# Recurrent stage of an AdaLN / attention / FFN kernel: skip term and residual as products on TensorE, copies and first taps on ScalarE, start and tail reordered

## What is computed

```python
xn = h * rsqrt(mean(h * h, -1) + 1e-6) * rms_w
proj = xn @ in_proj_W.T + in_proj_b                 # z, K (two parts), V
vc = causal depthwise conv of V, 4 taps
u = silu(vc + conv_b)
dyn, sel_B, sel_C, seldt, beta, gates = u @ ...     # per head: the "heads"
Y = scan over the 1024 steps (2x2 rotation, rank-1 correction)
y = sum(Q * Y)
y = groupnorm(y) over 16 channels x all steps, times gn_w, plus gn_b
y = y * silu(z)
y = y + D * u                                       # the skip term
branch = h + y @ out_W.T                            # h is folded elsewhere
x = x + branch                                      # the residual
```

## Time and profile before

| | us |
|---|---|
| median of 3 runs (lowest to highest) | 2272.09 (2267.52 to 2276.97) |
| the profiled execution | 2275.35 |
| its span in the profile | 2273.6 |
| TensorE, VectorE, ScalarE busy in the span | 1917.5, 1596.7, 886.0 |

### The profile page before, as it was taken

The page is one execution under the profiler, slowest core; times in us unless marked ns, Lnnn a source line. Parts: engine busy times, 40 slices in busy tenths (PEclk is TensorE's granted clock), DMA queues, the critical chain, the costliest instruction groups (busy, mean ns, idle before and its releaser), DMA issues. The chain is left out here.

```text
span 2273.6 us, 28338 instructions
## 1 busy us (share of the span) xinstructions
PE 1917.5 (84%) x9864; PEld 1237.0 (54%) x9864; DVE 1596.7 (70%) x3420; ACT 886.0 (39%) x1659; POOL 461.5 (20%) x350
## 2 busy tenths in 40 slices
PE   7999998999999987956865377455889999999997
PEld 4544443788888855433433233232354444379997
DVE  4688873545444354789999999999467888266775
ACT  2366764222232222530122111101326776446775
POOL 1021210433230030001001101110011221114775
PEclk9899988999999998978887788777988999979999
DMA  6033332211010011000000000000032342138885
GB/s 182 13 73 65 66 64 80 84 56 56 32 42 0 0 56 66 26 1 10 10 1 9 19 0 10 9 0 0 24 57 43 74 82 49 35 116 238 231 235 121
DMA packets 60158, 132.73 MB, mean 58 GB/s; under 512 B 18952, under 2 KB 29960, under 8 KB 57216
## 3 DMA queue, kind: packets, MB, share of 16 engines
q1 hardware_dynamic: 50688, 118.17, 19.2%
q0 software_dynamic: 8832, 12.16, 3.2%
q10 hardware_dynamic: 512, 0.79, 0.2%
HBM read 91.27 MB, written 10.98 MB: 45 GB/s over the span
## 5 line engine op out<-in xcount | busy, mean ns | idle before, releaser
L810 DVE CUSTOM_DVE_ANT_0 pair<-pair,a_mask 128x512 f32<-128x512 f32 (+3 forms) x768 | 407.3, 588 | 108.6 <-PE pair L621 106.4
L776 ACT ACTIVATE a_prob<-pair 128x512 f32<-128x512 f32 (+3 forms) x768 | 330.3, 491 | 174.7 <-PE pair L648 172.6
L621 PE MATMUL pair<-a_kx,a_qx 48*128 48x512 f32 (+3 forms) x768 | 246.6, 411 | 15.9 <-DVE a_mx_raw L810 8.9
L648 PE MATMUL pair<-a_qx,a_kx 64*128 64x512 f32 (+3 forms) x768 | 248.3, 432 | 9.2 <-ACT a_prob L776 9.2
L648 PEld LDWEIGHTS pair<-a_qx,a_kx 64*128 64x128 f32 x768 | 119.0, 197 | 186.7 <-ACT a_prob L776 135.6
L1079 DVE TENSOR_TENSOR m_h<-pair,m_g 128x512 f32<-128x512 f32 x96 | 66.3, 691 | 205.0 <-PE pair L870 202.1
L1466 PE MATMUL pair<-h_stream,r_w_kz 128*128 128x512 f32 x192 | 103.7, 694 | 118.8 <-DVE r_region L1872 113.4
L868 PE MATMUL pair<-m_x_hi,m_w_lo 128*128 128x512 f32 x448 | 178.8, 399 | 19.3 <-DVE m_w_lo L1042 6.4
L662 PE MATMUL pair<-a_prob,a_v 128*32 128x512 f32 (+3 forms) x1536 | 177.6, 536 | 6.5 <-ACT a_prob L776 4.0
L869 PE MATMUL pair<-m_x_hi,m_w_hi 128*128 128x512 f32 x448 | 177.6, 396 | 0.0
L870 PE MATMUL pair<-m_x_lo,m_w_hi 128*128 128x512 f32 x448 | 177.1, 395 | 0.0
(11 more groups left out here) (323 smaller groups left out, 4080.2 us busy)
## 6 DMA issues: line engine op xcount, KB each, us to landing
mx_raw<-in_L_ffn_experts SPq DMA_DIRECT2D x69, 512.0 KB
comp_or_raw<-in_L_cond_experts SPq DMA_DIRECT2D x18, 1024.0 KB, 5.0
a_factor<-a_inverses SPq DMA_DIRECT2D x56, 128.0 KB, 2.7
a_qx<-comp_or_raw SPq DMA_DIRECT2D x52, 96.0 KB, 2.7
a_qx<-a_comp SPq DMA_DIRECT2D x52, 96.0 KB, 2.7
a_kx<-comp_or_raw SPq DMA_DIRECT2D x24, 192.0 KB, 4.5
a_kx<-a_comp SPq DMA_DIRECT2D x24, 192.0 KB, 4.5
r_w_ring<-in_r_q_w SPq DMA_DIRECT2D x8, 512.0 KB, 3.9
```

The lines of the kernel that those rows point to most:

```text
L621: nc.tensor.matmul(first_bank[t % FR][:, 0:c1 - c0], qx[r, m % 2, a // 2, i * P:(i + 1) * P], kx[r, m % 3, a // 2, c0:c1], start=True, sto ...
L648: nc.tensor.matmul(score_bank[t % SR][:, q0:TT], kx[r, n % 3, a // 2, j * P:(j + 1) * P], qx[r, n % 2, a // 2, h * TT + q0:(h + 1) * TT], ...
L776: nc.scalar.activation(prob[:, i % RING, a, q0:TT], score_bank[t % SR][:, q0:TT], ACT.Exp, scale=SCALE).then_inc(s["b_exp"], 1)
L810: nc.vector.tensor_tensor_reduce(out=first_bank[t % FR][:, 0:cols], in0=first_bank[t % FR][:, 0:cols], in1=mask[:, m0:m0 + cols], scale=1. ...
```

## The change

- **Skip term.** L1964 goes, so a gate is one operation and counts `fin` once. In unit 4 ScalarE scales a copy of the output weights by D (`w_skip`, four operations), and TensorE adds D * u through it: four more products per result tile.
- **Residual.** One more product per tile, identity times x (read by step), starts each sum. ScalarE copies the finished tile back into x, by step, in place of VectorE's add. For batch 1 the identity and skip products are tiles of their own, `("skip", 1, o, h)`, late in unit 5's ring, copied to x by ScalarE; the y part is still added at the end.
- **First taps.** `first_tap` on ScalarE, right after `evict_v`, replaces L1755.
- **Start.** Two of the four squares go to VectorE. **Tail.** `result(0, 0)`, `result(0, 1)`, `result(1, 0)` are issued when half 0 of the last outputs is read, ahead of the first group sum; `result(1, 1)` between the group sums.

```diff
@@ -1258,7 +1258,7 @@
 READ = 2 * HALF_T
-TAPS = 1 + 2 * (TG - 1)
+TAPS = 2 * (TG - 1)
@@ -1281,6 +1281,8 @@
             tiles += [("out", 0, o, h) for o in range(KD) for h in halves]
+        if r == KI + 1:
+            tiles += [("skip", 1, o, h) for o in range(KD) for h in halves]
         rings.append(tiles)
@@ -1288,7 +1290,7 @@
 RING_ALL = [tile for tiles in RINGS for tile in tiles]
-BY_DVE = ("gn1", "out")
+BY_DVE = ("gn1",)
@@ -1308,7 +1310,7 @@
     names = ("norms const vload hload sload kload qload oload sq gp ga gd rc xn pad acc u h1 h2 cb cd cp x1 qc d1 ya "
-             "as st fin ai oadd omm dt dt2 tail").split()
+             "as st fin ai oadd omm dt dt2 tail tap skip_w").split()
     s = {n: c.sem(f"r_{n}") for n in names}
@@ -1341,6 +1343,7 @@
         w_o = tmp[:, 0:4, :].rearrange("p a t -> p (a t)").rearrange("p (k m) -> p k m", k=KI)
+        w_skip = tmp[:, 4:8, :].rearrange("p a t -> p (a t)").rearrange("p (k m) -> p k m", k=KI)
         values = [*c.quad, *[bank[:, :] for bank in c.bank]]
@@ -1429,7 +1432,7 @@
                     for i, tile in enumerate(tiles):
-                        if (tile[0] == "out") != late:
+                        if (tile[0] in ("out", "skip")) != late:
                             continue
@@ -1481,11 +1484,17 @@
                             b, o, h = which
-                            pe.wait_ge(s["oload"], 16)
-                            pe.wait_ge(s["fin"], 2 * KI)
+                            pe.wait_ge(s["skip_w"], KI)
+                            nc.tensor.matmul(bank.rearrange("p (g i) -> p g i", g=2), c.ident[:, :], by_step(c.x, b, o, h),
+                                             start=True, stop=False)
                             for k in range(KI):
-                                last = nc.tensor.matmul(bank, w_o[:, k, o * P:(o + 1) * P], ybuf[:, k, half(h)],
-                                                        start=k == 0, stop=k == KI - 1)
+                                last = nc.tensor.matmul(bank, w_skip[:, k, o * P:(o + 1) * P], u[:, b, k, half(h)],
+                                                        start=False, stop=what == "skip" and k == KI - 1)
+                            if what == "out":
+                                pe.wait_ge(s["fin"], KI)
+                                for k in range(KI):
+                                    last = nc.tensor.matmul(bank, w_o[:, k, o * P:(o + 1) * P], ybuf[:, k, half(h)],
+                                                            start=False, stop=k == KI - 1)
                         last.then_inc(s["gp"], 1)
@@ -1539,19 +1548,22 @@
                 def result(k, o):
-                    pe.wait_ge(s["fin"], 2 * (KI + k + 1))
+                    pe.wait_ge(s["fin"], KI + k + 1)
                     for h in range(HALF_T):
...
+                pe.wait_ge(s["d1"], (NU - 1) * READ + 2)
+                result(0, 0)
+                result(0, 1)
+                result(1, 0)
                 pe.wait_ge(s["d1"], NU * READ)
-                result(0, 0)
                 group_sum(("gn1", NU - 1))
-                result(0, 1)
+                result(1, 1)
                 group_sum(("gn2", NU - 1))
-                for k in range(1, KI):
+                for k in range(2, KI):
                     for o in range(KD):
@@ -1573,6 +1585,11 @@
                                              bias=in_bias[:, m:m + 1]).then_inc(s["ga"], 1)
+
+                def first_tap(b, m):
+                    act.wait_ge(s["ga"], taken(("v", b, m, HALF_T - 1))[1])
+                    nc.scalar.activation(u[:, b, m, :].rearrange("p (g i) -> p g i", g=TG), vpad[b][:, m, :, 1:GT + 1], ACT.Identity,
+                                         scale=vecs[:, m, 3:4]).then_inc(s["tap"], 1)
@@ -1591,7 +1608,7 @@
                     if r >= 2:
-                        act.wait_ge(s["fin"], 2 * (r - 1))
+                        act.wait_ge(s["fin"], r - 1)
                     for h in range(HALF_T):
@@ -1674,18 +1691,19 @@
-                for b in range(B):
-                    for k in range(KD):
-                        nc.scalar.activation(squares[:, b * KD + k, :], seq(c.h, b)[:, k, :], ACT.Square).then_inc(s["sq"], 1)
+                for k in range(KD):
+                    nc.scalar.activation(squares[:, k, :], seq(c.h, 0)[:, k, :], ACT.Square).then_inc(s["sq"], 1)
                 act.wait_ge(s["norms"], 2 * 16)
...
                     evict_v(0, m)
+                    first_tap(0, m)
                 evict_k(0)
...
                     evict_v(1, m)
+                    first_tap(1, m)
                     silu_u(0, m)
@@ -1707,6 +1725,17 @@
                         normalize(r - 1)
+                    if r == KI:
+                        act.wait_ge(s["oload"], 16)
+                        for k in range(KI):
+                            nc.scalar.activation(w_skip[:, k, :], w_o[:, k, :], ACT.Identity, scale=vecs[:, k, 7:8])\
+                                .then_inc(s["skip_w"], 1)
+                    if r in (KI, KI + 1):
+                        for o in range(KD):
+                            for h in range(HALF_T):
+                                tile = ("out", 0, o, h) if r == KI else ("skip", 1, o, h)
+                                nc.scalar.activation(by_step(c.x, tile[1], o, h), tile_in(tile).rearrange("p (g i) -> p g i", g=2),
+                                                     ACT.Copy).then_inc(s["ga"], 1)
                     for i in LATER_HEADS.get(r, ()):
@@ -1732,7 +1761,7 @@
                         if r and h == HALF_T - 1:
-                            pool.wait_ge(s["fin"], 2 * r)
+                            pool.wait_ge(s["fin"], r)
                         tt(ybuf[:, m, half(h)], coef[:, 2, half(h)], coef[:, 5, half(h)], ALU.add).then_inc(s["ya"], 1)
@@ -1750,12 +1779,12 @@
                 def convolve(b, m):
-                    dve.wait_ge(s["ga"], taken(("v", b, m, HALF_T - 1))[1])
                     v, out = vpad[b][:, m, :, :], u[:, b, m, :].rearrange("p (g i) -> p g i", g=TG)
-                    ts(out, v[:, :, 1:GT + 1], vecs[:, m, 3:4], None, ALU.mult).then_inc(s["acc"], 1)
+                    dve.wait_ge(s["tap"], b * KI + m + 1)
                     for back in range(1, TG):
                         w = vecs[:, m, 3 - back:4 - back]
-                        dve.wait_ge(s["acc"], (b * KI + m) * TAPS + 2 * back - 1)
+                        if back > 1:
+                            dve.wait_ge(s["acc"], (b * KI + m) * TAPS + 2 * (back - 1))
                         for to, src in ((out[:, back:TG, :], v[:, 0:TG - back, 1:GT + 1]),
@@ -1960,9 +1989,6 @@
                     tt(ybuf[:, m, :], ybuf[:, m, :], zbuf[:, r % 2, :], ALU.mult).then_inc(s["fin"], 1)
-                    dve.wait_ge(s["fin"], 2 * r + 1)
-                    stt(out=ybuf[:, m, :], in0=u[:, b, m, :], scalar=vecs[:, m, 7:8], in1=ybuf[:, m, :],
-                        op0=ALU.mult, op1=ALU.add).then_inc(s["fin"], 1)
@@ -1980,13 +2006,6 @@
                         down(level)
-                        if r == KI and level == 1:
-                            for o in range(KD):
-                                for h in range(HALF_T):
-                                    dve.wait_ge(s["gp"], made(("out", 0, o, h)))
-                                    x = by_step(c.x, 0, o, h)
-                                    tt(x, ring_bank(("out", 0, o, h)).rearrange("p (g i) -> p g i", g=2), x, ALU.add)\
-                                        .then_inc(s["gd"], 1)
                         if later and level == 4:
@@ -2002,6 +2021,9 @@
+                for k in range(KD):
+                    h1 = seq(c.h, 1)[:, k, :]
+                    nc.vector.tensor_tensor(squares[:, KD + k, :], h1, h1, ALU.mult).then_inc(s["sq"], 1)
                 for b in range(B):
@@ -2030,6 +2052,7 @@
                 gate(NU - 1)
+                dve.wait_ge(s["ga"], taken(("skip", 1, KD - 1, HALF_T - 1))[1])
                 for o in range(KD):
```

## The result

The changed kernel measured 2284.04 us (median of 18 runs, 2278.04 to 2295.59), the kernel before 2276.02 in 18 runs beside it; the ratio is 1.0051, 95% interval [1.003, 1.0072], where the two medians alone stand 8.0 us or 0.35% apart. Both intervals lie above 1, so the changed kernel is slower, by half to three quarters of a per cent. The 2283.3 us of the forecast lies close, but by its steps it was worse than that looks, as the stage shows.

What follows compares the result with a forecast made beforehand. TensorE was taken to bound the joints and VectorE the scan between them. Terms 9.6 + 2.9 - 0.3 + 2.1 - 3.1 = +11.2 us on the 2272.09 us median gave 2283.3 us, range 2274 to 2292.

Steps and rivals of the forecast that it cites:

- the bound and its places: Joints belong to TensorE, the scan between to VectorE; VectorE waits some 18 us in unit 4, 5 in unit 5.
- Rival 4: Unit 4: added products hide in TensorE's idle time, -9.7 us or -14.5 with joints, 2257 to 2262 us; chance 0.03.
- units 4 and 5: Added products delay the half-1 queries VectorE waits for: +9.6 us in unit 4, +2.9 us in unit 5.
- all added products have this size: Units 4 and 5: every product added to TensorE is priced as 512 columns of fp32, 0.86 us each.
- rival 1: Units 4 and 5: identity products' reads by step slow, +3.5 us, +6.9 at a doubling, 2287 to 2290; chance 0.31.
- Start: Stage start: taps on ScalarE delay head products 1.1 us, low clock costs 1.8, one tap gives -0.75; sum +2.1 us.
- rival 2: Stage start: the clock holds and the pause stays short, -2.2 us instead of +2.1, 2279 us; chance 0.12.
- Other joints and tail: Four lighter gates at other joints give -0.3 us; fewer result products left at the end give -3.1 us.
- The 4.6 us at the low clock: Tail: first group sum stands behind six result products, low clock for the first 4.6 us; 1590.3 against 1590.38.
- The sum: Whole kernel: 9.6 + 2.9 - 0.3 + 2.1 - 3.1 = +11.2 us, put on the median: 2283.3 us.
- 0.43 us a product: Behind unit 5: without the 13.43 us pause, 40 spread records take 0.43 us a product, not 11.38 us for 20.

Runs made afterwards that it cites:

- the second set: The changed kernel, unedited, measured again against the kernel before: 2290.03 us (12 runs; before 2276.76), ratio 1.0074.
- the kernel of 699.8 us: Kernel before with split squares, one first tap on ScalarE, unit 4's adds moved down, reordered end, POOL's gate wait lifted; ratios 0.9985 and 0.996.

## Why the prediction was right or wrong

- **Right: the bound and its places.** The joints are TensorE's (the run without D * u), the added products all stand ahead of a reader that waits, and the two waits lie where they were put. Without the step VectorE's wait in unit 4 is 17.94 us for 18 forecast. Rival 4, that the products hide, needed 14 us or less; the queue is 35.
- **Wrong in size: units 4 and 5.** The step that failed is "all added products have this size", 0.86 us. It holds for the 48 skip and y products; the eight identity products read by step and take 1.79. Unit 4 is +13.1 for +9.6, unit 5 +7.0 for +2.9. Both differences (3.5 and 4.1) are nearly four times 0.93, 3.7. This was rival 1 at its doubling, with 6.9 us forecast and 6.7 to 7.0 measured. The chance of 0.31 was too low: the only rows by step there were, VectorE's, said 1.5, and the forecast took 1. The Trainium skill (SBUF — State Buffer, Door 1: The DMA port swizzle) wants two hits on a 16-byte line, and by that rule such a read is slow, as it was: 1.79 us for 0.86. The same section lets fp32 be read by a step of four for free, which these numbers contradict; the measurement decides. Whether missing second hits are the cause, no run here shows.
- **Start, +1.0 for +2.1.** Right in kind: the mean comes 1.5 us earlier (2.44 us into the stage for 3.95), ScalarE's chain then holds the heads up, the pause is 4.33 us (5 forecast), and the heads lose 1.7 to the clock (1.8 forecast). ScalarE was better than assumed: a round of eviction, tap and Silu takes 3.37 us (928.12 to 931.49), not 3.5, and its table load came 1.1 us earlier in the stage rather than 0.5. So the heads start 0.1 us late, not 1.1. With the taps back on VectorE the pause is 1.91 us, the clock is 1.00 and the first coefficient comes 2.3 to 2.5 us earlier than before the change (3.2 with one tap on ScalarE): rival 2's gain was to be had, only not with eight taps on ScalarE.
- **Other joints and tail.** -0.5 for -0.3 and -3.4 for -3.1: as forecast. The first group sum comes 4.7 us after the last read and was 5.1, so reordering ahead of it is nearly free, as the prediction argued. The 4.6 us at the low clock that the prediction counted there stand in no row of the kernel before; the first 12 records ran 7.06 us at a granted clock of 0.74, by which some 3.7 us were at the low level.
- **The sum.** The steps make +17.1 on the stage for +11.2 forecast. (Its +9.6 for unit 4 is 9.5 by its own terms, 1377.3 less 1367.83.) The measured ratios, 0.51% and 0.74% of 2276, are 12 and 17 us. That the first median lies 0.7 us from the forecast is luck: the kernel before measured 3.9 us more in that set than the 2272.09 the forecast was put on, and the two medians differ by 8.0 us where the stage differs by 17. The stage and the second set (2290.03) say rival 1, 2290.
- **Missed.** The sum counted 0.43 us a product for the spreads behind unit 5, from the absent pause, and so had the clock's gain in it. It did not ask what the same effect is worth with a smaller load: the split in two units gains it twice with almost no wait (0.36 us), together with the operation that leaves the gate.

## What to carry to other kernels

Before work moves from a busy engine to an idle one, look which of them arrives last at the joint, not which is busier: here 10 us of VectorE's work removed gave 1 us, and 20 products more in a queue of 16 cost 13. A queue in order makes the place of added work matter more than its amount: the same 20 products cost 7 us in one unit and gained 3.5 when split over two units whose idle time held them. Where two engines arrive within a microsecond of each other, as in those joints, the gain takes both of them: the faster spreads and the lighter gate. And price an operand by its own layout, not by the size of the product.

## What the hardware showed beyond expectation

- A 512-column fp32 product whose moving operand is read every fourth value takes 1.79 us from start to start against 0.86 read plainly (same weights, same line; the same tile read plainly by other products takes 0.86 too). ScalarE's copy to every fourth value takes 1.08 us against 0.69 for a plain eviction of 512 columns, or 0.63 a piece for two in a row.
- The clock's loss after a pause is paid by what stands behind the joint: 40 spread records take 9.24 us at a granted clock of 1.00 after 1.35 to 1.54 us of pause, and 11.3 to 11.4 at 0.78 to 0.79 after 13.4. A longer pause does not cost more: behind 25.57 us, ahead of unit 4, they take 10.56 us at 0.86. Real work in the pause, with one operation less in VectorE's gate, shortened units 5 and 6 together by 3.5 us.
- After the long pause ahead of the tail (15.2 us) the clock came back one group of products later in two of three profiles with the same tail (the kernel before again, and its adds moved); this moves the tail by 3.1 us.
- Run beside each other, an add of POOL and an operation of VectorE took longer: in the tail of the kernel of 699.8 us POOL's second half of y takes 2.18 us (1.26 before) while VectorE's D * u operation takes 2.17 (1.29 before). No run here shows the cause.
